# Layer 0's feed-forward stage by token tile in a two-layer graph transformer kernel (one core)

## What is computed

```python
h = layernorm(x)                       # (384, 1024)
def act_quant(x):                      # of rmsnorm(x), per row
    scale = 127.0 / clip(max(abs(x)), 1e-05)
    q = clip(round(x * scale), -128, 127) / scale
def weight_quant(w):
    scale = 1.0 / clip(mean(abs(w)), 1e-05)
    q = clip(round(w * scale), -1, 1) / scale
bitlinear(x, w, b) = act_quant(rmsnorm(x)) @ weight_quant(w).T + b
x = x + bitlinear(gelu(bitlinear(h, w1, b1)), w2, b2)      # 1024 -> 512 -> 1024
xn = layernorm(x); x1 = xn @ W1 + b1 ...                    # layer 1 (g1 and on)
```

## Time and profile before

| what | value |
|---|---|
| median of 3 runs | 865.74 us (864.54 to 867.39) |
| the profiled execution, its time | 872.22 us |
| its span | 870.5 us |
| mean granted TensorE clock | 0.971 of full |
| busy: VectorE, ScalarE, POOL | 602.4, 367.9, 93.3 us |
| the chain that ended last, by engine | TensorE 65%, VectorE 22%, ScalarE 5%, DMA 3% |
| HBM read | 91.99 MB, 107 GB/s over the span |

### The profile page before, as it was taken

The page is one execution under the profiler, slowest core; times in us unless marked ns, Lnnn a source line. Parts: engine busy times, 40 slices in busy tenths (PEclk is TensorE's granted clock), DMA queues, the critical chain, the costliest instruction groups (busy, mean ns, idle before and its releaser), DMA issues.

```text
span 870.5 us, 11581 instructions
## 1 busy us (share of the span) xinstructions
PE 802.1 (92%) x4313; PEld 701.7 (81%) x4315; DVE 602.4 (69%) x1223; ACT 367.9 (42%) x789; POOL 93.3 (11%) x92
## 2 busy tenths in 40 slices
PE   5899999899998999988994599989998988999998
PEld 4788878799998999976872288868777878999886
DVE  8888879755546788884687767777886575666241
ACT  4222222463435666652443045484565123464220
POOL 3000019400000000011002102010001121000000
PEclk9999999999999999999996789999999999999999
DMA  5421232433333322289443237533223235234440
GB/s 184 159 69 56 71 115 81 138 102 122 99 132 105 107 92 68 60 292 259 164 150 73 72 100 171 155 118 122 97 73 116 78 91 145 73 124 143 145 133 36
DMA packets 28775, 102.17 MB, mean 117 GB/s; under 512 B 3736, under 2 KB 3864, under 8 KB 28464
## 3 DMA queue, kind: packets, MB, share of 16 engines
q1 hardware_dynamic: 24928, 88.85, 29.8%
q0 software_dynamic: 3792, 12.59, 7.3%
HBM read 91.99 MB, written 1.57 MB: 107 GB/s over the span
## 4 chain that ended last, share of the span: by engine, by line
PE 65%; DVE 22%; ACT 5%; issue 4%; DMA 3%; POOL 1%; SPq 0%; DVEq 0%; ACTq 0%
PE bank L1764 24%; PE bank L1812 24%; PE bank L1662 6%; DVE w_lo L1077 5%; DMA raw<-weights 3%; PE bank L1711 3%; DVE prob L1469 1%; PE bank L1713 1%; PE bank L1854 1%; DVE stats L1092 1%; ACT kf L869 1%; DVE v L1066 1%; PE bank L1670 1%; ACT w_hi L838 1%; DVE probT L1066 1%
## 5 line engine op out<-in xcount | busy, mean ns | idle before, releaser
L1077 DVE TENSOR_TENSOR w_lo<-raw,w_hi 128x1024 fp32r<-128x1024 f32 x140 | 183.6, 1320 | 88.5 <-ACT w_hi L838 88.1
L838 ACT ACTIVATE w_hi<-raw 128x1024 fp32r<-128x1024 f32 x140 | 147.5, 1056 | 150.6 <-PE bank L1812 91.0
L1764 PE MATMUL bank<-xn1T,w_hi 128*128 128x384 f32 x448 | 115.2, 338 | 0.4 <-DVE xn1T L1066 0.4
L1812 PE MATMUL bank<-w_hi,xn3T 128*128 128x512 f32 x336 | 108.1, 395 | 0.0
L1764 PEld LDWEIGHTS bank<-xn1T,w_hi 128*128 128x128 f32 x448 | 79.9, 188 | 1.4 <-DVE w_lo L1077 0.6
L1764 PE MATMUL bank<-xn1T,w_lo 128*128 128x384 f32 x224 | 75.0, 335 | 0.0
L1812 PEld LDWEIGHTS bank<-w_hi,xn3T 128*128 128x128 f32 x336 | 63.6, 189 | 13.3 <-issue 0.3
L1764 PE MATMUL bank<-xn4T,w_hi 128*128 128x384 f32 x256 | 65.2, 335 | 2.2 <-DVE xn4T L1066 2.2
L1812 PE MATMUL bank<-w_lo,xn3T 128*128 128x512 f32 x168 | 65.8, 392 | 0.0
L1764 PEld LDWEIGHTS bank<-xn4T,w_hi 128*128 128x128 f32 x256 | 46.0, 188 | 2.4 <-issue 2.4
L1764 PE MATMUL bank<-xn4T,w_lo 128*128 128x384 f32 x128 | 42.8, 334 | 0.0
(11 more groups left out here) (338 smaller groups left out, 1723.5 us busy)
## 6 DMA issues: line engine op xcount, KB each, us to landing
raw<-weights SPq DMA_DIRECT2D x140, 512.0 KB, 3.2
row_sb<-rows SPq DMA_DIRECT2D x6, 512.0 KB, 5.6
kcat<-kcat POOLq DMA_DIRECT2D x16, 192.0 KB, 3.0
base<-rows POOLq DMA_DIRECT2D x6, 512.0 KB, 10.8
w2r<-w_in SPq DMA_DIRECT2D x1, 2048.0 KB, 11.9
w1r<-w_in SPq DMA_DIRECT2D x1, 2048.0 KB, 8.7
x_sb<-x_in SPq DMA_DIRECT2D x3, 512.0 KB, 4.4
row_sb<-rows SPq DMA_DIRECT2D x6, 256.0 KB, 5.2
```

The lines of the kernel that those rows point to most:

```text
L838: act.activation(w_hi[:, u % RING], raw[:, u % RAW], ACT.Copy).then_inc(hi_split, 1)
L1077: dve.tensor_tensor(w_lo[:, u % RING], raw[:, u % RAW], f(w_hi[:, u % RING]), ALU.subtract).then_inc(unit_split, 1)
L1764: last = pe.matmul(out_of(pr)[:, 0:N], w[pa][:, slot, k * P:(k + 1) * P], TT[src][:, pb, k], start=(k == 0 and m == 0), stop=(k == KD - 1 ...
L1812: last = pe.matmul(out_of(pr)[:], tile[:, pa, k, ts], w[pb][:, at_, j * HALF:(j + 1) * HALF], start=(kk == 0 and j == 0 and m == 0 and nam ...
```

## The change

The step `ffn` is replaced by one step for each part and tile, written into the list by hand, between the last four units of `wo`'s second half and of `g1`, which TensorE now takes tile by tile (`tile` steps; `BY_TILE`, `TILED` = 4). For those units the splits come in `ahead_hi` (ScalarE), `ahead_lo` (VectorE) and `ahead` steps, not at the unit (`held`). The row scale for quantisation is taken from the largest |x - mean| alone, since the norms' factor cancels; the norms' power goes only into the factor back (`quant_back`). Clipping is done before the transposes. ScalarE does the scaling of `xn2`, the casts of `w2` (from VectorE), `w1` and `hq`, empties the transposes, and applies the layer norm (`x_norm`). A gelu of one column (`gelu_table`) stands behind `wo`'s first tile. POOL, not SP, issues `w1r`, in step `attend 15`, and POOL adds base1 into base2 tile by tile. The memset of `ctx1` moves from `g1` 1 to `q` 0.

```diff
...
     steps.append(("ffn_mean", 1))
-    run("wo", 5, 8)
+    run("wo", 5, 7)
+    steps.append(("w_cast", 1))
     steps.append(("ffn_abs", 0))
-    run("wo", 8, 9)
+    run("wo", 7, 12)
     steps.append(("ffn_mean", 0))
-    run("wo", 9, 12)
-    steps.append(("ffn",))
-    steps.append(("transpose", "xn3"))
+    def tiled(name, c, t, a=0, b=TILED):
+        return ("tile", name, c, t, a, b)
+    steps.extend([tiled("wo", 1, 0), ("gelu_table",), tiled("wo", 1, 1), ("in_stats", 0), ("w_cast", 0), ("in_amax", 0),
+                  tiled("wo", 1, 2, 0, 2), ("in_factor", 0), ("in_stats", 1), ("in_scale", 0), ("in_round", 0),
+                  tiled("wo", 1, 2, 2, 4), ("ahead_hi",), ("in_amax", 1), ("ahead_hi",), ("in_factor", 1), ("in_T", 0),
+                  ("in_stats", 2), ("in_scale", 1), ("in_ev", 0), ("in_amax", 2), ("ahead_hi",), ("ffn_h", 0),
+                  ("in_factor", 2), ("in_round", 1), ("in_scale", 2), ("in_round", 2), ("in_T", 1), ("hn", 0), ("in_ev", 1),
+                  ("in_T", 2), ("ahead_lo",), ("gelu", 0), ("ffn_h", 1), ("square", 0), ("h_max", 0), ("in_ev", 2),
+                  ("h_factor", 0), ("h_round", 0), ("ahead_hi",), ("ffn_h", 2), ("hn", 1), ("h_cast", 0), ("ahead_lo",),
+                  ("gelu", 1), ("square", 1), ("h_max", 1), ("h_T", 0), ("hn", 2), ("h_ev", 0), ("h_factor", 1), ("gelu", 2),
+                  ("h_round", 1), ("ffn_o", 0), ("square", 2), ("h_max", 2), ("h_cast", 1), ("h_factor", 2), ("h_round", 2),
+                  ("h_T", 1), ("h_cast", 2), ("x_out", 0), ("h_ev", 1), ("h_T", 2), ("ffn_o", 1), ("h_ev", 2), ("ffn_o", 2),
+                  ("x_out", 1), ("x_norm", 0), ("xn3_T", 0), ("ahead_lo",), ("xn3_hi", 0), ("ahead_lo",), ("x_norm", 1),
+                  ("xn3_lo", 0), ("xn3_T", 1), ("x_out", 2)])
     run("g1", 0, 4)
+    steps.extend([tiled("g1", 0, 0, 0, 2), ("xn3_hi", 1), ("xn3_lo", 1), tiled("g1", 0, 0, 2, 4), ("x_norm", 2), ("xn3_T", 2),
+                  tiled("g1", 0, 1, 0, 2), ("xn3_hi", 2), ("xn3_lo", 2), tiled("g1", 0, 1, 2, 4), ("g1_out", 0),
+                  tiled("g1", 0, 2, 0, 2), tiled("g1", 0, 2, 2, 4), ("g1_out", 1), ("ahead",), ("ahead",), ("g1_out", 2)])
 
...
-STAGGERED = (("wo", 1), ("wp", 1), ("e2", 1))
+STAGGERED = (("wp", 1), ("e2", 1))
+BY_TILE = (("wo", 1), ("g1", 0))
+def held(name, i):
+    return by_tile(name, i) and (name, i) != ("wo", 12 - TILED)
...
-                    if (name, i) == ("wo", 7):
-                        wait_full(sp, "attend.15")
-                        sp.dma_start(w1r[:], w1_in).then_inc(ffn_landed[0], 16)
...
+                if s[0] == "in_stats":
+                    t = s[1]
+                    pool.wait_ge(in_var, t + 1)
+                    link(pool.tensor_scalar(power_in[:, t:t + 1], mv[:, t, 1:2], 1.0 + EPS, EPS * EPS, ALU.mult, ALU.add))
+                    pool.tensor_tensor(q_s[:, 1, t:t + 1], power_in[:, t:t + 1], minus_half[:, 0:1], ALU.pow).then_inc(in_power, 1)
+                    pool.wait_ge(b2_landed, 16 * NT)
+                    pool.dma_start(base2[:, t], base1[:, t], accum_op=ALU.add).then_inc(base2_ready[t], 16)
+                if s[0] == "square":
+                    t = s[1]
+                    pool.wait_ge(sq_ready, t + 1)
+                    power(h_s[:, 1, t:t + 1], h_s[:, 0, t:t + 1], 1.0 / HID, 1).then_inc(rms_ready, 1)
+                if s[0] == "x_out":
+                    t = s[1]
+                    pool.wait_ge(ln_stats, NT + t + 1)
+                    link(power(rstd[:, t:t + 1], mv[:, t, 1:2], 1.0, 1))
+                    pool.tensor_scalar(shift[:, 1, t:t + 1], mv[:, t, 0:1], rstd[:, t:t + 1], -1.0, ALU.mult,
+                                       ALU.mult).then_inc(ln_rstd, 1)
...
+                    wait_full(pool, "attend.15")
+                    pool.dma_start(w1r[:], w1_in).then_inc(ffn_landed[0], 16)
...
+                if kind == "w_cast":
+                    w = s[1]
+                    src, dst = ((w1r, w1q), (w2r, w2q))[w]
+                    act.wait_ge(w_unit, 2 - w)
                     act.wait_ge(consts, 7)
-                    act.activation(w1q[:].rearrange("p a b -> p (a b)"), w1r[:], ACT.Identity,
-                                   bias=minus_round[:]).then_inc(w1_quant, 1)
...
+                    act.activation(dst[:].rearrange("p a b -> p (a b)"), src[:], ACT.Identity,
+                                   bias=minus_round[:]).then_inc(w_quant, 1)
+                if kind == "gelu_table":
+                    act.wait_ge(consts, 7)
+                    act.activation(junk[:, 0:1], minus_round[:], ACT.Gelu)
+                if kind == "in_scale":
+                    t = s[1]
+                    act.wait_ge(in_scaled, t + 1)
+                    act.activation(xn2[:, t], base1[:, t], ACT.Identity, bias=shift[:, 0, t:t + 1],
+                                   scale=q_s[:, 5, t:t + 1]).then_inc(in_nat, 1)
...
+                if kind == "h_cast":
+                    t = s[1]
+                    act.wait_ge(h_rounded, t + 1)
+                    act.activation(hq[:, t], hn[:, t], ACT.Identity, bias=minus_round[:]).then_inc(h_quant, 1)
...
+                if kind == "x_norm":
+                    t = s[1]
+                    act.wait_ge(ln_rstd, NT + t + 1)
+                    act.activation(xn3[:, t], x_sb[:, t], ACT.Identity, bias=shift[:, 1, t:t + 1],
+                                   scale=rstd[:, t:t + 1]).then_inc(nat_ready, 1)
...
+            def quant_rows(q, t, least):
+                one = slice(t, t + 1)
+                link(dve.tensor_scalar(q[:, 3, one], q[:, 2, one], least, 1.0 / 127.0, ALU.max, ALU.mult))
+                link(dve.reciprocal(q[:, 5, one], q[:, 3, one]))
+            def quant_back(q, w, t):
+                one = slice(t, t + 1)
+                note(dve.scalar_tensor_tensor(q[:, 6, one], q[:, 3, one], w_s[:, 1, w:w + 1], q[:, 1, one], ALU.mult, ALU.mult))
...
+                    dve.tensor_scalar(raw_w[:], raw_w[:], -1.0, ROUND, ALU.max, ALU.add).then_inc(w_unit, 1)
+                if kind == "in_stats":
+                    t = s[1]
+                    wo_out(1, t)
+                    noted()
+                    dve.bn_aggr(mv[:, t], stats[:, t]).then_inc(in_var, 1)
+                if kind == "in_amax":
+                    t = s[1]
+                    one, mean = slice(t, t + 1), mv[:, t, 0:1]
+                    wo_min(1, t)
+                    dve.wait_ge(in_var, t + 1)
+                    noted()
+                    note(dve.scalar_tensor_tensor(q_s[:, 2, one], span[:, 0, 0, one], span[:, 0, 1, one], mean, ALU.max, ALU.subtract))
+                    link(dve.scalar_tensor_tensor(q_s[:, 4, one], span[:, 1, 0, one], span[:, 1, 1, one], mean, ALU.min, ALU.subtract))
+                    link(dve.scalar_tensor_tensor(q_s[:, 2, one], q_s[:, 4, one], -1.0, q_s[:, 2, one], ALU.mult, ALU.max))
+                if kind == "in_factor":
+                    t = s[1]
+                    quant_rows(q_s, t, CLIP * EPS)
+                    dve.tensor_scalar(shift[:, 0, t:t + 1], mv[:, t, 0:1], q_s[:, 5, t:t + 1], -1.0, ALU.mult,
+                                      ALU.mult).then_inc(in_scaled, 1)
+                if kind == "in_round":
+                    t = s[1]
+                    dve.wait_ge(in_nat, t + 1)
+                    link(dve.tensor_scalar(xn2[:, t], xn2[:, t], ROUND, ROUND + 127.0, ALU.add, ALU.min))
+                    dve.tensor_scalar(xq[:, t], xn2[:, t], ROUND - 128.0, ROUND, ALU.max, ALU.subtract).then_inc(in_quant, 1)
+                    dve.wait_ge(in_power, t + 1)
+                    quant_back(q_s, 0, t)
...
+                if kind == "h_round":
+                    t = s[1]
+                    dve.wait_ge(sq_ready, t + 1)
+                    link(dve.tensor_scalar(hn[:, t], hn[:, t], h_s[:, 5, t:t + 1], ROUND, ALU.mult, ALU.add))
+                    dve.tensor_scalar(hn[:, t], hn[:, t], ROUND + 127.0, ROUND - 128.0, ALU.min, ALU.max).then_inc(h_rounded, 1)
+                if kind == "x_out":
+                    t = s[1]
+                    dve.wait_ge(rms_ready, t + 1)
+                    quant_back(h_s, 1, t)
+                    dve.wait_ge(base2_ready[t], 16)
+                    noted()
+                    for c in range(2):
+                        pr = f"ffn_o.{t}.{c}"
+                        sl = slice(c * HALF, (c + 1) * HALF)
+                        emptied(dve.scalar_tensor_tensor(x_sb[:, t, sl], out_of(pr)[:], h_s[:, 6, t:t + 1], base2[:, t, sl],
+                                                         ALU.mult, ALU.add), pr)
+                    for c in range(2):
+                        wait_emptied(dve, f"ffn_o.{t}.{c}")
+                        half_stats(x_sb, t, c)
+                    tile_stats(t)
...
+                if kind == "tile":
+                    _, name, c, t, first, end = s
+                    src, per = NODE_MAJOR[name]
+                    pr, ts = f"{name}.{c}.{t}", slice(t * P, (t + 1) * P)
```

(39 more changed lines are left out.)

336 lines of the change are left out of this document (137 added, 199 removed).

## The result

The changed kernel takes 852.87 us (median of 4 runs, 850.45 to 853.56), the kernel before 865.95 on the same chip (4 runs, 864.54 to 867.39). The ratio is 0.9846 (95% interval 0.9813 to 0.9878), so the change wins 1.5%, 13.1 us. The forecast was 853.7, the range 848.5 to 860.5. The profiled execution took 852.8 us with a span of 851.1.

The account below looks back on a forecast made before the run. TensorE was taken to bound the kernel, busy 802.1 of 870.5 us. Gains of 3.9 us at `w1r`, 14.4 at `g1`'s start and 12.0 at its end; the 12.0 off the 865.74 median gave 853.7, range 848.5 to 860.5.

Parts of the forecast that it names:

- To the scaled `w1r`: From the end of `attend.15`: earlier weight loads and `w2`'s cast on ScalarE scale `w1r` at 448.6, 3.9 us won.
- Quantisation: VectorE quantising the three tiles back to back: 15.1 us, from 448.6 to 463.7, ScalarE's work hidden.
- Hidden layer: VectorE's steps from 463.7 to 476.6: 10.7 us of work plus 2.2 us of waits.
- Output and norm: VectorE's steps from 476.6 to `g1`'s start at 488.8, including 2.1 us of waits; 14.4 us earlier than before.
- The clock: TensorE at its lower clock from 461 to 468, before `g1` and in its first 3.4 us; `g1` ends at 508.7.
- Behind `g1`: From `g1`'s end to the span's end: 349.8 us, unchanged.
- "`g1`" and its cover: `g1` takes 19.9 us; hop 0's dot products end 11 us after `q` starts, before TensorE wants them at 12.2.
- The gelu table: Table load of 1.28 us on ScalarE, moved to 442.2 where ScalarE is idle: hidden, cost zero.
- First rival: VectorE's passes over `w2r` hold POOL's issue of `w1r`, ScalarE's sum starts 5 us later: 858.7 us, 14%.
- by rows: POOL's writing time for `w1r` goes by its 128 rows: 0.9 us, over before VectorE's passes over `w2r`.
- by bytes: POOL's writing time for `w1r` goes by its bytes: 3.6 us, running into VectorE's passes over `w2r`.
- Second rival: POOL's transfers are slow regardless of VectorE: `w1r` takes 25.7 us and lands at 451.8; 869.0 us, 5%.

Follow-up runs that it names:

- Runs 2 and 3: Changed kernel with `w1r` back on SP's queue behind its old wait, 857.96 us; changed kernel with `w2`'s cast back on VectorE, 852.74 us.
- run 4: Changed kernel's operations and engines, but each feed-forward step done for all three tiles before the next; 869.09 us, ratio to before 1.0025.
- Run 9: Changed kernel plus 16 TensorE products that nothing reads, behind the transposes of `xn3` tile 0; 849.66 us, ratio to before 0.982.
- run 6: Changed kernel without the one-column gelu, so the table loads in front of the first real gelu; 855.54 us in one execution.
- run 5: Changed kernel with POOL issuing `w1r` only after VectorE has begun its passes over `w2r`; 862.64 us in one execution.

## Why the prediction was right

- **"To the scaled `w1r`"**: forecast 3.9 won (452.5 to 448.6), measured 4.2. Runs 2 and 3 confirm both causes, by 5.1 and 1.8 us at the scaled `w1r`. But run 4 has the same gain at `w1r` and is no faster than before.
- **"Quantisation"**: 15.1 us forecast, 15.2 measured (442.06 to 457.22). The only wait of VectorE was 0.38, for the product of `wo` tile 2.
- **"Hidden layer" and "Output and norm"**: `g1` at 487.6 against 488.8. ScalarE's wait for `g1` 3 was 2.03, as worked out; the 1.2 us that `hn` 1 was to wait for its product did not come, and `x_out` 0 began 1.1 earlier. The next part came out (12.1 us, forecast 12.2), but by another path: VectorE had none of the 2.1 us of waits that I allowed it. It was done with `xn3`'s low part of tile 0 at 478.84, and TensorE stood until 479.80 for tile 1's norm, which POOL, held by the two `w_lo`, gave 1.7 late, and then took 1.97 us for its transposes at the lower clock. These 2.6 us lie where my waits lay: luck, not insight.
- **"The clock"** was low for less time than I said, and this sign of being right did not show: I had a mean under 0.8 from 461 to 488, and it was 0.89. On that axis the low stretches were within 471 to 476 and 486 to 489, where I had 461 to 468 and 3.4 us of `g1`. The layout ended at 504.6 with the upper level throughout and I took 508.7, 4.1 more; `g1` ended at 505.8, 2.9 earlier. But the clock explains only part of these 2.9: 1.1 were won before `x_out` 0, half of it the wait that did not come, and 1.7 within `g1`, which took 18.2 us and not 19.9. Of the 1.7, 0.9 are waits that I allowed `g1` and that did not come, and some 0.7 are the clock, which cost about 1.0 there and not 1.7. Run 9 measures 1.4 for the clock around `g1`'s start, its transposes included; for the low stretch at 465 to 470 of after no run tells its price.
- **Behind `g1`**: forecast 349.8 us to the span's end as before, measured 351.5. The 1.6 more is again the clock, at 599. The two errors, 2.9 and 1.7, are of opposite sign, so the total, 853.7 against 852.87, looks better than its terms: part of that is luck.
- **"`g1`" and its cover**: hop 0's dot products end at 510.52, 10.9 us after `g1` (11 forecast), and TensorE takes the row at 511.66 without a wait.
- **"The gelu table"**: zero, by run 6. After's own stands at 435.66, and ScalarE is idle for 4.94 us behind it.
- **First rival**: the mechanism exists (run 5). There it went with 7.3 us lost in the stretch, where I gave 5.0, but that run also issues later. The changed kernel is outside it since the issue of 2 MB in 128 rows took 0.55 us. Of my two readings "by rows" (0.9) is near and "by bytes" (3.6) is not.
- **Second rival**: `w1r` landed 8.9 us after POOL's issue, not 25.7.
